# A two-layer attention and feed-forward kernel: late row vectors loaded early, column sums of the last weight moved one tile on, 40 idle products at the front

## The chip, the cores and the metric

The kernel runs on one core of one Trainium2 chip. A core has a matrix engine (PE, TensorE; its weight loads are shown apart as PEld), a vector engine (DVE), a scalar engine (ACT), a general engine (POOL, GpSimd) and a queue engine (SP) that issues DMAs. The engines run their own instruction lists side by side and wait for one another by semaphores. The metric is the device time of one execution in microseconds (us); lower is better.

## The reference

The input is 8 tiles of 128 tokens with 256 features, with a context of the same shape. Four blocks are added to it in turn, each on the layer-normalised input.

```python
x = x + _L0_xattn_ref(_layernorm(x), ctx, theta_w, ..., out_w, out_b)   # attention over 256 columns, latent 64
x = x + _L0_ffn_ref(_layernorm(x), w_gate, w_up, w_down)                # silu(gate)*up, Hadamard, 8-bit x ternary
x = x + _L1_xattn_ref(_layernorm(x), ctx, Wq, bq, Wkv, bkv, Wp, bp)     # 16 heads, 1024 queries x 1024 keys
x = x + _L1_ffn_ref(_layernorm(x), w1, b1, gamma, beta, w2, b2)

def _L1_ffn_ref(x, w1, b1, gamma, beta, w2, b2):
    h = bitlinear(x, w1, b1)
    h = jax.nn.gelu(h, approximate=False)
    h = layernorm(h, gamma, beta)          # gamma and beta are 1024 long
    return bitlinear(h, w2, b2)            # ternary w2
```

The rounded numbers of the last product carry an offset of 128. It is taken off with the column sums of the ternary W2, which have to be known before the last stage.

## The kernel before

Everything is kept in on-chip memory, and each engine has one instruction list in an order written out by hand. The stages follow one another, with some overlap:

- **First stage** (about 0 to 80 us): loads, first layer norm, first attention, and the key and value projections of the second attention from the context. `ctx_transposes(j)` turns the context of pair j of tiles (buffer `cx`), `project(j)` and `values1(j)` multiply the normalised input, `k_project` and `v_project` read the K/V weights (`wkvs`). GpSimd adds `xs` and `cx` in `x_plus_ctx`.
- **Gate stage** (about 80 to 125 us) and the Hadamard and down products that follow it. ACT sums and rounds the weights (`w_sums`, `w_round`), which come in through two slots of `stage`; SP issues the loads of w_down, w1 and w2 when a slot comes free (`sp.wait_ge(w_int, ...)`).
- **Second attention** (about 173 to 370 us): a loop over u from 0 to 127, u = 16 t + h for tile t and head h. For each u, PE computes the scores of 128 queries by 1024 keys in two products of 512 columns (`scores(u)`, L1928, once `exp` of u - 3 is done), DVE takes the negated maximum (`nm`, L1385), POOL makes the bias (`eb`, L581), ACT takes the exponential (L908). The result is turned either by a DMA transpose that SP issues (`turn(u)`, L402) or, for heads 1, 4, 12 and 15 of tiles 1 to 7, by PE (`round_transposes(u)`, L1940) and ACT (`move(u)`, L895). Seven heads later PE multiplies it with the values (`attend`, L1955). Query tiles are turned in between (`q_transposes`, L1725, and `qT_out`, L879): those of tile 7 at u = 17 through bank 7 (`N_BANK`), which the column sums and the PE transposes of the heads also use.
- **Last stage**: the wide product with W1, gelu, second layer norm with gamma and beta, the product with W2.

`wide_rows` holds b1, gamma and beta, 1024 numbers each, and is spread over all 128 partitions: 1.5 MB in on-chip memory. SP issues that one DMA in the attention loop, behind the turns up to u = 20 (L412), into a part of `rb` that the query quantisation has left. GpSimd reads b1 from u = 36 on (`b1_part`), DVE reads gamma and beta in the last stage.

The column sums of W2 are eight products on PE at u = `W2_SUMS` = 18 (L1845), behind a wait for `q_tr_sb` = 8, which is the copy of the last turned query tile on ACT. DVE scales them at u = 19 (`w2_correction`, L1424), and PE waits for that at u = 20 before it uses bank 7 again. The code of that part of the PE loop is this:

```python
                if u == W2_SUMS:
                    pe.wait_ge(q_tr_sb, T)
                    column_sums(W2, N_BANK, c2_ps)
                if u == H + ON_TENSOR[0] + TR_LAG:
                    pe.wait_ge(c2_sb, 1)
```

Of the kernel before, what the change touches and what calls it, by code (L numbers as in the profile page):

```python
# [23 lines left out]
P = 128  # L24
T = 8
NP = T // 2
D = 256
F = 1024
# [3 lines left out]
H = 16  # L32
# [14 lines left out]
TR_LAG = 3  # L47
# [7 lines left out]
T_BANK, D_BANK, N_BANK, Q_BANK = 4, 5, 7, 6  # L55
LATE_Q = {11: 5, 14: 6, 17: 7}
FIRST_ATTENDED = {9: (0, 1), 10: (2, 3), 11: (4,), 12: (5,), 13: (6,)}
W2_SUMS = 18
SUM_LAG = 3
PROJ_LAG = 14  # L60
O_OUT_LAG = 8
# [8 lines left out]
SUM_BANK, SCALE_BANK, XQ_BANK = 0, 2, 4  # L70
GATE_BANKS = (4, 5, 0, 1)
UP_BANKS = (6, 7, 2, 3)
ROWS = ["bq", "bk", "bp", "b2"]
WIDE_ROWS = ["b1", "gamma", "beta"]

# [44 lines left out]
def build(nc, x, ctx_in, att_w, out_w, gam_bet, cols, ident, hada, blk, rows, wide_rows, w_gate, w_up, w_down,  # L120
          wq, wkv, wp, w1, w2, out):
    with ExitStack() as stack:
# [82 lines left out]
        qz = [rb[:, 1024 * b:1024 * b + 1024].bitcast(BF16).rearrange("p (j e n) -> p j e n", e=2, n=P) for b in range(2)]  # L205
        osb = rb[:, 2048:4096].rearrange("p (t n) -> p t n", t=T)
        oT = rb[:, 7168:7680].rearrange("p (b c n) -> p b c n", b=2, c=2)
        wide = rb[:, 4096:7168]
        rowv.update({n: wide[:, F * i:F * i + F] for i, n in enumerate(WIDE_ROWS)})

        hw = [ra[:, F * t:F * t + F] for t in range(T)]
        squares = rb[:, 0:512].bitcast(BF16)
# [53 lines left out]
        def bank(b, n=1):  # L266
            return ps[:, b * 512:(b + n) * 512]
# [93 lines left out]
        def wslot(i):  # L361
            return stage[:, i % 2, :]
# [7 lines left out]
        @block.sync  # L370
        def _(sp):
            sp.dma_start(attw[:, :], att_w).then_inc(ld_att, 16)
            for j in range(NP):
                sp.dma_start(pair(xs, j), pair(x_d, j)).then_inc(ld_x[j], 16)
                sp.dma_start(pair(cx, j), pair(c_d, j)).then_inc(ld_c[j], 16)
            sp.dma_start(gb[:, :, :], gam_bet).then_inc(ld_const, 16)
            sp.dma_start(outw[:, :], out_w).then_inc(ld_const, 16)
            sp.dma_start(half_mean[:, :], blk).then_inc(ld_const, 16)
            sp.dma_start(wkvs[:, :, :], wkv).then_inc(ld_kvw, 16)
            sp.dma_start(h128[:, :], hada).then_inc(ld_const, 16)  # L380
            for i in range(2):
                sp.dma_start(wslot(i), w_d[i]).then_inc(ld_w[i], 16)
            sp.dma_start(wqs[:, :, :], wq).then_inc(ld_qpw, 16)
            sp.dma_start(wps[:, :, :], wp).then_inc(ld_qpw, 16)
            for i in range(2, 5):
                sp.wait_ge(w_int, i - 1)
                sp.dma_start(wslot(i), w_d[i]).then_inc(ld_w[i], 16)
            sp.wait_ge(qz_zero, 1)

            def pad_queries(t):  # L390
                sp.wait_ge(q_tr_sb, t + 1)
                if t >= 2:
                    sp.wait_ge(s_ps, H * (t - 1))
                for e in range(2):
                    r = slice(SLOT * e, SLOT * e + SLOT)
                    sp.dma_start(qz[t % 2][r, :, e, :], qT[r, t, :, :]).then_inc(q_pad[t % 2], 16)

            def turn(u):
                sp.wait_ge(s_exp, u + 1)
                if u >= R_RING:  # L400
                    sp.wait_ge(s_av, u - R_RING + 1)
                sp.dma_start_transpose(rT[u % R_RING].rearrange("p (c n) -> p c n", c=T),  # L402
                                       esc[u % E_RING].bitcast(F16)).then_inc(s_turned[u % R_RING], 16)

            pad_queries(0)
            pad_queries(1)
            for u in range(U):
                if not by_tensor(u):
                    turn(u)
                if u == H + 4:  # L410
                    sp.wait_ge(q_tr_sb, T)
                    sp.dma_start(wide, wide_rows.to_broadcast([P, wide.shape[1]])).then_inc(ld_wide, 16)  # L412
                if u % H == 1 and 2 <= u // H + 1 < T:
                    pad_queries(u // H + 1)
            for t in range(T):
                sp.wait_ge(f_out, t + 1)
                sp.dma_start(o_d[:, t, :], xn[:, t, :]).then_inc(out_done, 16)
            sp.wait_ge(out_done, 16 * T)
# [3 lines left out]
        def _(pool):  # L422
# [118 lines left out]
            def b1_part(step, piece):  # L541
# [1 line left out]
                c = slice(D * piece, D * piece + D)  # L543
                x, y = bwork[:, 0, :], bwork[:, 1, :]
                if step == 0:
                    pool.wait_ge(ld_wide, 16)
                    pool.wait_ge(w_tern, 5)
                    ins = nc.gpsimd.tensor_copy(bpart[:, c], rowv["b1"][:, c])
                elif step in (1, 4):
# [487 lines left out]
        def _(dve):  # L1037
# [432 lines left out]
            q_quant4(3)  # L1470
            for u in range(9, U + O_LAG):
                attention(u)
                if u == W2_SUMS + 1:
                    w2_correction()


# [54 lines left out]
            xqT_out(2, NP + 2, token_bank(2))  # L1531
            o_sums(T - 1)
            o_scale(T - 1)
            dve.wait_ge(ld_wide, 16)
            f_centre(0)
            f_scales(0)
            o_residual(T - 1)
# [28 lines left out]
        def _(pe):  # L1566
# [170 lines left out]
            def w_total(i, b):  # L1737

                pe.wait_ge(w_abs, i + 1)
                M(b[:, i:i + 1], ones[:, :], wsum[:, i:i + 1], start=True, stop=True).then_inc(w_tot, 1)  # L1740

            ctx_transposes(0)
            ctx_transposes(1)
            project(0)
            values1(0)
# [162 lines left out]
            def q_transposes(t):  # L1908
                n_bank_read()
                pe.wait_ge(q_four, t + 1)  # L1910
                head_transposes(t, q4[(t // 2) % 2], bank16(N_BANK), q_tr)
                in_n_bank[1] += 1
# [175 lines left out]
            for u in range(9, U + AV_LAG):  # L2088
                if u < U:
                    scores(u)  # L2090
                if u in LATE_Q:
                    q_transposes(LATE_Q[u])
                if u == W2_SUMS:
                    pe.wait_ge(q_tr_sb, T)
                    column_sums(W2, N_BANK, c2_ps)
                if u == H + ON_TENSOR[0] + TR_LAG:
                    pe.wait_ge(c2_sb, 1)
                if u - TR_LAG < U and by_tensor(u - TR_LAG):
                    round_transposes(u - TR_LAG)
# [100 lines left out]
```

## Time and profile before

| what | value |
|---|---|
| time, three runs | 419.59, 421.86, 423.8 us (median 421.86) |
| the profiled execution: its time | 422.52 us |
| the profiled execution: its span | 420.7 us |
| outside the span | 1.82 us |
| mean granted TensorE clock | 0.862 |
| busy: PE, DVE, ACT, POOL | 313.3, 350.7, 321.6, 126.0 us |

The span goes from the first to the last instruction of the core in one profiled execution. All durations below are from that execution. Busy time is a sum over the whole span. No engine is busy all the time, and each stage has its own limit, so it says little about one stage.

### The profile page before, as it was taken

How to read it: one execution, taken by the hardware profiler on the slowest of the kernel's cores; microseconds unless marked ns; L12 is line 12 of the kernel's file. 1: busy time of each engine (PE TensorE's matmuls, PEld its weight loads, DVE VectorE, ACT ScalarE, POOL GpSimd, SP SyncE). 2: the span in 40 equal slices, each digit the busy share in tenths (PEclk: the TensorE clock that was granted, in tenths of full speed). 3: DMA queues.
4: the chain of work that ended last, by engine and by line, in shares of the span. 5: the costliest groups of instructions: out<-in, count | busy, mean ns of one | idle time of the engine just before them, and what ended most of it. 6: DMA issues, size and time to landing. Idle time of an engine off the chain costs nothing.

```text
span 420.7 us, 7501 instructions
## 1 busy us (share of the span) xinstructions
PE 313.3 (74%) x2597; PEld 190.7 (45%) x2597; DVE 350.7 (83%) x562; ACT 321.6 (76%) x523; POOL 126.0 (30%) x303
## 2 busy tenths in 40 slices
PE   3989997674657698766587777777687766888967
PEld 2756554421256587444343444443444443533434
DVE  4658999379999888779588999989999999779885
ACT  2676689854205858979879998999999999887851
POOL 5333534200010220312211456532322232247330
PEclk9969999589558799888979997999989998995576
DMA  8800032000002002256989897989888978900001
GB/s 276 332 2 2 2 100 100 2 0 1 0 2 100 2 0 50 52 101 129 153 226 189 164 158 138 171 136 161 162 150 151 158 145 133 145 2 14 12 25 51
DMA packets 119862, 40.97 MB, mean 97 GB/s; under 512 B 114704, under 2 KB 118416, under 8 KB 119056
## 3 DMA queue, kind: packets, MB, share of 16 engines
q1 hardware_dynamic: 119392, 39.89, 47.4%
q8 instruction: 21, 0.34, 0.4%
q0 software_dynamic: 144, 0.52, 0.3%
q14 instruction: 17, 0.14, 0.1%
q10 hardware_dynamic: 288, 0.07, 0.1%
HBM read 11.11 MB, written 1.05 MB: 29 GB/s over the span
## 4 chain that ended last, share of the span: by engine, by line
DVE 27%; PE 25%; ACT 24%; issue 18%; DMA 3%; POOL 2%; SPq 0%; DVEq 0%; ACTq 0%; POOLq 0%
ACT rb L908 15%; DVE nm L1385 4%; PE ps L1928 3%; PE ps L2033 3%; PE ps L1990 2%; DVE rb L1303 2%; PE ps L1904 2%; PE ps L1940 2%; DVE gs L1294 2%; DMA tern<-rb 2%; DVE rb L1316 1%; DVE st L1048 1%; PE ps L1824 1%; DVE rb L1314 1%; PE ps L1835 1%
## 5 line engine op out<-in xcount | busy, mean ns | idle before, releaser
L1385 DVE TENSOR_REDUCE nm<-ps 128x1 f32<-128x1024 f32 x128 | 153.3, 1218 | 16.8 <-PE ps L1928 15.8
L908 ACT ACTIVATE rb<-ps,eb,sq 128x1024 int16<-128x1024 f32 x128 | 153.7, 1216 | 11.2 <-POOL eb L581 10.8
L1928 PE MATMUL ps<-ra,rb 128*128 128x512 bf16 x256 | 83.9, 413 | 43.4 <-ACT rb L908 42.8
L581 POOL TENSOR_SCALAR eb<-nm,sq 128x1 f32<-128x1 f32 x128 | 34.2, 267 | 126.4 <-DVE nm L1385 125.3
L1928 PEld LDWEIGHTS ps<-ra,rb 128*128 128x128 bf16 x256 | 15.8, 99 | 61.7 <-ACT rb L908 59.7
L1955 PEld LDWEIGHTS ps<-ra,tern 128*128 128x128 f16 x624 | 25.0, 98 | 16.8 <-issue 4.9
L1955 PE MATMUL ps<-ra,tern 128*128 128x16 f16 x624 | 25.8, 171 | 2.9 <-DVE rb L1123 2.3
L1824 PE MATMUL ps<-xqT,tern 128*128 128x512 bf16 x64 | 20.3, 464 | 9.8 <-DVE rb L1303 8.5
L908 ACT ACTIVATION_READ_ACCUMULATOR rb<-ps,eb,sq 128x1 f32 x128 | 27.3, 213 | 0.0
L771 ACT ACTIVATE sl<-gs 128x512 f32<-128x512 f32 x16 | 9.8, 626 | 17.6 <-DVE rb L1303 15.0
L1940 PEld LDWEIGHTS ps<-idh,rb 128*128 128x128 f16 x224 | 15.6, 106 | 16.1 <-issue 10.1
L1940 PE MATMUL ps<-idh,rb 128*128 128x128 f16 x224 | 19.0, 234 | 4.8 <-issue 2.5
L778 ACT ACTIVATE sB<-ps,shift,small 128x1024 uint8<-128x1024 f32 x8 | 9.6, 1204 | 15.4 <-DVE small L1334 15.4
L1955 PEld LDWEIGHTS ps<-ra,stage 128*128 128x128 f16 x400 | 16.0, 97 | 8.6 <-issue 1.1
L1294 DVE TENSOR_TENSOR gs<-ps,sB 128x512 f32<-128x512 f32 x16 | 11.0, 686 | 7.3 <-issue 5.1
L1824 PEld LDWEIGHTS ps<-xqT,tern 128*128 128x128 bf16 x64 | 6.2, 112 | 23.2 <-DVE rb L1303 14.6
L1955 PE MATMUL ps<-ra,stage 128*128 128x16 f16 x400 | 16.5, 170 | 0.0
L1835 PE MATMUL ps<-h,ra 128*128 128x128 f32 x64 | 10.9, 348 | 4.1 <-DVE ra L1316 4.1
L524 POOL TENSOR_SCALAR ve<-mv 128x2 f32<-128x2 f32 x4 | 1.3, 323 | 41.8 <-DVE mv L1051 41.8
L1725 PE MATMUL ps<-idb,rb 128*128 128x128 bf16 x128 | 11.0, 236 | 2.8 <-ACT ra L716 1.0
L1990 PE MATMUL ps<-tern,xqT 128*128 128x512 bf16 x32 | 13.1, 503 | 0.0
L1725 PEld LDWEIGHTS ps<-idb,rb 128*128 128x128 bf16 x128 | 8.9, 107 | 8.0 <-issue 4.6
(236 smaller groups left out, 727.9 us busy)
## 6 DMA issues: line engine op xcount, KB each, us to landing
stage<-w SPq DMA_DIRECT2D x2, 1024.0 KB, 4.7
rb<-ra SPq DMA_DIRECT2D x16, 128.0 KB, 2.9
rb<-wide_rows SPq DMA_DIRECT2D x1, 1536.0 KB, 7.1
xs<-x SPq DMA_DIRECT2D x4, 256.0 KB, 4.9
cx<-ctx_in SPq DMA_DIRECT2D x4, 256.0 KB, 5.2
stage<-w_gate SPq DMA_DIRECT2D x1, 1024.0 KB, 7.9
stage<-w_up SPq DMA_DIRECT2D x1, 1024.0 KB, 10.6
stage<-w_down SPq DMA_DIRECT2D x1, 1024.0 KB, 4.8
```

The source lines that it names most:

```text
L581: nc.gpsimd.tensor_scalar(eb[:, u % 3:u % 3 + 1], nm[:, u % 3:u % 3 + 1], sq[:, t, h:h + 1], LN255, ALU.mult, ALU.add).then_inc(s_bias, 1)
L908: A(esc[u % E_RING], bank(2 * (u % 3), 2), ACT.Exp, bias=eb[:, u % 3:u % 3 + 1], scale=sq[:, t, h:h + 1], accum_out=es[:, t % 2, h:h + 1]) ...
L1294: V.tensor_tensor(gs[:, n % 2, :], bank(GATE_BANKS[n % 4]), sB[:, 512 * hf:512 * hf + 512], ALU.mult).then_inc(g_scaled, 1)
L1385: V.tensor_reduce(nm[:, u % 3:u % 3 + 1], bank(2 * (u % 3), 2), AX.X, ALU.max, negate=True).then_inc(s_max, 1)
L1725: ins = TR(b[:, jj * P:jj * P + P], src[:, o:o + P], idb[:, :])
L1824: ins = M(bank(b[n % 4]), tern[:, w, F * k + P * c:F * k + P * c + P], xqT[:, k, 512 * hf:512 * hf + 512], start=(k == 0), stop=(k == 1))
L1835: ins = M(bank(2 * (t % 2), 2)[:, P * c:P * c + P], mixes[hf][:, c, P * (t % 4):P * (t % 4) + P], h128[:, :], start=True, stop=True)
L1928: ins = M(bank(2 * (u % 3) + hf), qz[t % 2][:, h // 2, h % 2, :], kT[:, h // 2, 512 * hf:512 * hf + 512], start=True, stop=True)
L1940: ins = TR(half_bank(7)[:, P * c:P * c + P], esc[u % E_RING].bitcast(F16)[:, P * c:P * c + P], idh[:, :])
L1955: ins = M(bank(6)[:, HD * h:HD * h + HD], rT[u % R_RING][:, P * c:P * c + P], vq[:, c, HD * h:HD * h + HD], start=(c == 0), stop=(c == T - 1))
L1990: ins = M(b, xqT[:, k, P * t:P * t + P], tern[:, W1, F * k + 512 * hf:F * k + 512 * hf + 512], start=False, stop=(k == 1))
L2033: ins = M(b, fT16[:, t % 2, P * c:P * c + P], w[:, D * c:D * c + D], start=False, stop=(c == FC - 1))
```

## The change

It does three things.

1. The DMA of `wide_rows` is taken out of the attention loop and split in two. b1 goes to `wkvs`, once the key and value projections are done; gamma and beta go to `cx`, once the context has been turned, added and projected. SP issues both directly behind the load of w_down and ahead of that of w1, with five waits. The readers wait for 32 instead of 16 on `ld_wide` and read from the new places.
2. `W2_SUMS` goes from 18 to 43, head 11 of tile 2. The wait for `q_tr_sb` moves to u = 20, where the wait for `c2_sb` stood; that wait moves to u = 47. The sums wait for the copy of the turned attention output of tile 1 (`o_tr_sb` = 2). DVE scales them at u = 46, behind the residual of tile 1.
3. Ahead of the first context transposes PE does 34 products of a 128 by 128 matrix of ones with itself into bank 5, which nothing reads, and 6 more between the first and the second pair.

```diff
-W2_SUMS = 18
+W2_SUMS = 43
...
+SPARE_BANK = 5
...
-        wide = rb[:, 4096:7168]
-        rowv.update({n: wide[:, F * i:F * i + F] for i, n in enumerate(WIDE_ROWS)})
+        wide_b1 = wkvs[:, :, :].rearrange("p k n -> p (k n)")
+        wide_gb = cx[:, :, :].rearrange("p t d -> p (t d)")
+        rowv.update({"b1": wide_b1, "gamma": wide_gb[:, 0:F], "beta": wide_gb[:, F:2 * F]})
...
             for i in range(2, 5):
                 sp.wait_ge(w_int, i - 1)
                 sp.dma_start(wslot(i), w_d[i]).then_inc(ld_w[i], 16)
+                if i == 2:
+                    sp.wait_ge(v_ps, 4)
+                    sp.wait_ge(k_ps, NP)
+                    sp.dma_start(wide_b1, wide_rows[:, 0:F].to_broadcast([P, F])).then_inc(ld_wide, 16)
+                    sp.wait_ge(xc_set, NP)
+                    sp.wait_ge(a_g, NP)
+                    sp.wait_ge(c_t, NP)
+                    sp.dma_start(wide_gb, wide_rows[:, F:3 * F].to_broadcast([P, 2 * F])).then_inc(ld_wide, 16)
...
-                if u == H + 4:
-                    sp.wait_ge(q_tr_sb, T)
-                    sp.dma_start(wide, wide_rows.to_broadcast([P, wide.shape[1]])).then_inc(ld_wide, 16)
...
-                if u == W2_SUMS + 1:
+                if u == W2_SUMS + 3:
                     w2_correction()
...
+            def keep_busy(n):
+
+                for i in range(n):
+                    M(bank(SPARE_BANK)[:, 0:P], one16[:, :], one16[:, :], start=True, stop=True)
+
+            pe.wait_ge(shift_set, 1)
+            keep_busy(34)
             ctx_transposes(0)
+            keep_busy(6)
             ctx_transposes(1)
...
+                if u == H + ON_TENSOR[0] + TR_LAG:
+                    pe.wait_ge(q_tr_sb, T)
                 if u == W2_SUMS:
-                    pe.wait_ge(q_tr_sb, T)
+                    pe.wait_ge(o_tr_sb, u // H)
                     column_sums(W2, N_BANK, c2_ps)
-                if u == H + ON_TENSOR[0] + TR_LAG:
+                if u == W2_SUMS + 4:
                     pe.wait_ge(c2_sb, 1)
```

PE's list at u = 18 and 19, before. The products `ps<-ra,rb` are scores, `ps<-ra,tern` are attended heads, `ps<-tern,one` the column sums.

```order
L1928 MATMUL ps<-ra,rb 128x512 [waits s_exp]
L1928 MATMUL ps<-ra,rb 128x512
L1845 MATMUL ps<-tern,one 1x256 [waits shift_set,w_tern,q_tr_sb]
L1845 MATMUL ps<-tern,one 1x256 x7
L1955 MATMUL ps<-ra,tern 128x16 [waits s_turned1]
L1955 MATMUL ps<-ra,tern 128x16 x7
L1928 MATMUL ps<-ra,rb 128x512 [waits s_exp]
```

The same place after:

```order
L1943 MATMUL ps<-ra,rb 128x512 [waits s_exp]
L1943 MATMUL ps<-ra,rb 128x512
L1970 MATMUL ps<-ra,tern 128x16 [waits s_turned1]
L1970 MATMUL ps<-ra,tern 128x16 x7
L1943 MATMUL ps<-ra,rb 128x512 [waits s_exp]
```

The eight sums and their wait are gone from between two pairs of scores. PE's list at u = 43 and 44, after:

```order
L1943 MATMUL ps<-ra,rb 128x512 [waits s_exp]
L1943 MATMUL ps<-ra,rb 128x512
L1860 MATMUL ps<-tern,one 1x256 [waits shift_set,w_tern,o_tr_sb]
L1860 MATMUL ps<-tern,one 1x256 x7
L1970 MATMUL ps<-ra,stage 128x16 [waits s_moved]
L1970 MATMUL ps<-ra,stage 128x16 x7
L1943 MATMUL ps<-ra,rb 128x512 [waits s_exp]
```

They stand here now, again between two pairs of scores; before, nothing stood between the second and the fifth of these rows. SP's list from the load of w_down on, after:

```order
L389 DMA stage<-w_down 128x2048 [waits w_int]
L393 DMA wkvs<-wide_rows 128x1024 [waits k_ps,v_ps]
L397 DMA cx<-wide_rows 128x2048 [waits c_t,a_g,xc_set]
L389 DMA stage<-w 128x2048 [waits w_int] x2
L406 DMA rb<-ra 64x8x128 [waits q_tr_sb,qz_zero]
```

Both new loads stand ahead of the loads of w1 and w2; before, the first and the fourth row were neighbours.

## Rows read from the trace of the kernel before

**Rows 1.** Profile page: busy engines; the chain that ended last, by engine.

```profile
PE 313.3 (74%) x2597; PEld 190.7 (45%) x2597; DVE 350.7 (83%) x562; ACT 321.6 (76%) x523; POOL 126.0 (30%) x303
DVE 27%; PE 25%; ACT 24%; issue 18%; DMA 3%; POOL 2%; SPq 0%; DVEq 0%; ACTq 0%; POOLq 0%
```

**Rows 2.** Timeline at u = 18 to 20: start, us, engine, line, what, [idle before].

```profile
206.99 1.07 ACT L879 ACTIVATE ra<-ps 128x1024 bf16<-128x1024 bf16 x1
207.89 1.26 ACT L908 ACTIVATE rb<-ps,eb,sq 128x1024 int16<-128x1024 f32 x1
208.11 1.03 PE L1845 MATMUL ps<-tern,one 128*1 128x256 f16 x8 [2.68 <-ACT ra L879]
...
209.29 0.84 PE L1928 MATMUL ps<-ra,rb 128*128 128x512 bf16 x2
...
210.17 1.23 DVE L1385 TENSOR_REDUCE nm<-ps 128x1 f32<-128x1024 f32 x1 [3.48 <-PE ps L1928]
...
211.47 0.35 DVE L1424 TENSOR_SCALAR half_mean<-ps 1x256 f16<-1x256 f32 x1
...
211.79 1.20 ACT L908 ACTIVATE rb<-ps,eb,sq 128x1024 int16<-128x1024 f32 x1 [2.55 <-POOL eb L581]
...
211.88 1.04 PE L1940 MATMUL ps<-idh,rb 128*128 128x128 f16 x8 [0.68 <-DVE half_mean L1424]
```

**Rows 3.** Timeline: exponentials of heads 6 and 14 of tile 1.

```profile
216.83 1.20 ACT L908 ACTIVATE rb<-ps,eb,sq 128x1024 int16<-128x1024 f32 x1
...
227.85 1.20 ACT L908 ACTIVATE rb<-ps,eb,sq 128x1024 int16<-128x1024 f32 x1 [0.62 <-POOL eb L581]
```

**Rows 4.** Timeline: exponentials of heads 2, 6 and 14 of tile 2.

```profile
233.64 1.21 ACT L908 ACTIVATE rb<-ps,eb,sq 128x1024 int16<-128x1024 f32 x1
...
238.84 1.24 ACT L908 ACTIVATE rb<-ps,eb,sq 128x1024 int16<-128x1024 f32 x1
...
249.26 1.20 ACT L908 ACTIVATE rb<-ps,eb,sq 128x1024 int16<-128x1024 f32 x1
```

**Rows 5.** DMA issues of the page (KB, median us to landing).

```profile
rb<-wide_rows SPq DMA_DIRECT2D x1, 1536.0 KB, 7.1
```

**Rows 6.** The DMA transposes (L402): time to landing.

```profile
DMA to landing us min/median/max: 3.1/3.3/6.4
```

**Rows 7.** Timeline of SP and PE behind the issue of the wide load at 214.40.

```profile
216.96 9.31 SPq L402 DMA_TRANSPOSE tern<-rb  x5
...
224.87 0.36 PE L1955 MATMUL ps<-ra,tern 128*128 128x16 f16 x8 [0.59 <-DMA tern<-rb]
```

**Rows 8.** Timeline at u = 44 to 47: PE, DVE.

```profile
244.55 0.60 PE L1928 MATMUL ps<-ra,rb 128*128 128x512 bf16 x2 [0.67 <-ACT rb L908]
...
245.19 3.60 DVE L1385 TENSOR_REDUCE nm<-ps 128x1 f32<-128x1024 f32 x3 [0.23 <-PE ps L1928]
```

**Rows 9.** Timeline of the first 13 us.

```profile
1.09 0.20 POOL L445 MEMSET one<- 128x128 f16 x1
...
6.25 1.09 PE L1676 MATMUL ps<-idf,cx 128*128 128x128 f32 x4 [6.25 <-DMA cx<-ctx_in]
...
7.76 1.09 PE L1676 MATMUL ps<-idf,cx 128*128 128x128 f32 x4 [0.42 <-DMA cx<-ctx_in]
...
8.78 1.12 PE L1580 MATMUL ps<-cx,attw 128*64 128x256 f32 x4
...
...
12.21 0.42 DVE L1064 COPY sB<-ps 128x256 f32<-128x256 f32 x1 [1.17 <-PE ps L1592]
```

**Rows 10.** Windows of 5 us: busy time of PE, PEld, DVE, ACT, POOL; PEclk; DMA share; GB/s.

```profile
25.00:30.00 5.00, 5.00 (x16) 3.41 (x14) 1.45 (x4) 2.58 (x10) 2.48 (x2) 0.52 0.01 3
...
210.00:215.00 5.00, 4.32 (x44) 2.31 (x43) 3.76 (x5) 2.97 (x5) 0.53 (x2) 0.50 0.72 131
```

**Rows 11.** Timeline: end of the last key projection; first use of w1.

```profile
66.83 1.13 PE L1718 MATMUL ps<-wkvs,rb 128*128 128x256 f32 x4
...
96.30 1.89 ACT L691 ACTIVATE tern<-stage 128x2048 bf16<-128x2048 f32 x1
```

More of the change, by code:

```diff
@@ L545, in b1_part @@
                 if step == 0:
-                    pool.wait_ge(ld_wide, 16)
+                    pool.wait_ge(ld_wide, 32)
                     pool.wait_ge(w_tern, 5)
@@ L1533, in _ @@
             o_scale(T - 1)
-            dve.wait_ge(ld_wide, 16)
+            dve.wait_ge(ld_wide, 32)
             f_centre(0)
```

## Prediction

> **What bounds the kernel now.** I read the page first. DVE is busy 83% of the span, ACT 76%, PE 74%, and the chain that ended last is shared by DVE, PE and ACT [rows 1]. So no engine bounds the whole, and the change touches three places. Each has to be read where it stands.
>
> The second attention is a stream of exponentials on ACT. The reader can measure a tile by the starts of the same heads. In tile 2, heads 2 to 14 start at 233.64 and 249.26, which is 15.62 us for twelve heads with two moves for PE's turns among them [rows 4]. In tile 1 the same heads start at 207.89 [rows 2] and 227.85 [rows 3], which is 19.96 us. The work is the same, so tile 1 loses 19.96 - 15.62 = 4.34 us between its heads 2 and 14. That is exactly the stretch with the column sums and the wide load.
>
> The timeline says how. PE has done the scores of u = 18 and stands for 2.68 us, until ACT has copied the last turned query tile (206.99 plus 1.07), and only then does the eight sums, 208.11 to 209.14. The scores of u = 19 come at 209.29 and take 0.84 us where a pair takes 0.60 at another place [rows 2, 8]. DVE stands for 3.48 us, ACT for 2.55 us; exponential 19 starts 3.90 us behind exponential 18. PE then waits once more, for DVE's scaled sums (0.68 us), and its granted clock is 0.50 in the window from 210 to 215, the lower of its two levels, 1.2 GHz [rows 2, 10].
>
> **The sums leave u = 18.** Heads 2 to 6 take 216.83 - 207.89 = 8.94 us in tile 1 and 238.84 - 233.64 = 5.20 us in tile 2 [rows 2 to 4]. The difference of 3.74 us is the wait, the sums, the second wait and the slow clock behind them. What is late next? The scores of u = 19 need exponential 16, which was over before the copy of 206.99 began, so they follow within half a microsecond of those of u = 18. DVE takes up their maximum behind that of 18. ACT's list has copy, exponential 18, exponential 19, which makes ACT itself the next limit, as in tile 2. The wait for the copy stands now ahead of PE's turn at u = 20. Queued behind it are the attended head and the scores of 21, whose release is exponential 18, over at 207.89 + 1.26 = 209.15; the copy is over at 208.06. So the moved wait costs nothing, and I take the whole 3.74 us. From below: if only ACT's own hole of 2.55 us closed, 2.6.
>
> **The wide load leaves the loop.** Heads 6 to 14 take 227.85 - 216.83 = 11.02 us in tile 1, 249.26 - 238.84 = 10.42 us in tile 2 [rows 3, 4]. The difference is 0.60 us. It is the wait of PE for a turned head at 224.87 (0.59 us), which ACT repeats as 0.62 us [rows 3, 7]. A DMA transpose lands after 3.3 us in the middle and 6.4 us at most [rows 6], and the longest stands behind the wide load, 1.5 MB with 7.1 us to landing [rows 5]. Gain 0.60; bounds 0 (the transposes stay late, see the rivals) and 0.60.
>
> **Where the load goes.** SP is in order, so behind its new waits stand the loads of w1 and w2. The last wait to be met is that for the key projection, whose products end at 66.83 + 1.13 = 67.96 [rows 11]. The two new loads together are as large as the old one; if they took its 7.1 us and w1 as much again behind them, w1 would be there at about 83 us with the issues. ACT first reads it at 96.30 [rows 11]. The load of w2 waits for a much later rounding. SP's list has no transpose before the second attention, so no head waits for these bytes. Cost nothing; the cover is the 13 us ahead of 96.30, and without it the gate stage would wait for what is missing. The readers of b1, gamma and beta change only their source buffer.
>
> **The sums arrive at u = 43.** Eight sums took 1.03 us [rows 2]. Ahead of the scores of u = 44 PE stands idle for 0.67 us, waiting for ACT [rows 8]. That hides 0.67, and 1.03 - 0.67 = 0.36 us is left. DVE stood idle 0.23 us ahead of that maximum because of PE and then runs three maxima without a hole [rows 8], so it has nothing to hide 0.36 with. At u = 46 it also gets the scaling, 0.35 us [rows 2], ahead of the maximum of 47; PE's turn at 47 waits for it, and behind that turn are an attended head and the scores of 48. The wait for `o_tr_sb` is met: that copy came on ACT at u = 40, and the scores of 43 already need exponential 40. Bounds 0 (ACT has slack at the move) and 0.36 + 0.35 = 0.71. I take 0.5, nearer to the upper end, since DVE ran without a hole there.
>
> **The 40 products at the front.** The ones are written at 1.09 + 0.20, the first context pair lands at 6.25, so PE has 5.0 us to itself [rows 9]. No row shows such products; the nearest is eight turns of 128 columns in f16 at the lower clock, 1.04 us, 0.13 each [rows 2]. 34 of them take 4.4 us and end at 5.8 us, ahead of 6.25. The six in between take 0.8 us at the lower clock; PE stands there 0.42 us for the second context pair anyway [rows 9], so they could delay it by 0.4 us. What can they bring? The four turns at 6.25 and at 7.76 took 1.09 us each, and the projection at 8.78 took 1.12 us: these are slow. DVE stands for 1.17 us at 12.21 because PE is late [rows 9], and that is all that the path can win here, for DVE's own list limits it next. So the bounds are a gain of 1.2 and a loss of 0.4. Against the full gain speaks that the clock does not stay: the kernel of before has it fall again in the window from 25 to 30 (0.52) although PE is busy there [rows 10], after a stretch with holes, and the front keeps a hole between 5.8 and 6.25 and one ahead of the projection. I take a gain of 0.3.
>
> **The sum.** 3.74 + 0.60 - 0.5 + 0.3 = 4.1 us off. The profiled execution took 422.52 us with a span of 420.7; that gives 418.4 and a span of 416.6. It stood 0.66 above the median of 421.86. Against the median the forecast is **417.8 us**.
>
> **Rivals.** (a) The transposes become the limit once tile 1 runs at ACT's pace. For it: five of them took SP 9.31 us, 1.86 each [rows 7], more than an exponential every 1.2 to 1.3 us, of which 12 in 16 go to SP. Against it: that was behind the wide load, and a head has seven heads' time until it is needed, over 8 us, against 3.3 to landing. Ten transposes late by 0.6 each, less 4.5 us of slack, give back 1.5 us: 419.3. The Trainium skill, page "DMA: Bandwidth & Descriptors", section "Latency and other measured facts", gives 261 GB/s for a DMA transpose; as an estimate from that page, one head of 0.26 MB would take 1.0 us, under the pace of ACT, which speaks against this rival; no run here shows the rate by itself.
>
> (b) The clock goes the other way in its favour. The front and the earlier stream shift PE's busy stretches, and the fall at 25 to 32 us does not come. There PE is busy 5.00 of 5 us [rows 10] and what it does would shrink by some 2 of them; with the front's 1.2 in place of 0.3 the sum is 4.1 + 0.9 + 1 = 6.0: 415.9. The same with the other sign, a fall more in the attention or the last stage and 1.5 us lost, gives 419.3.
>
> (c) Slower than before: each product of ones waits for the one ahead, since all write the same place of bank 5, and all 40 hold up the context. With p for one product, the projection starts at 1.3 + 40 p + 2 x 1.09 in place of 8.78, so the delay is 40 p - 5.3. It eats the other 3.8 us from p = 0.23 on; at 0.30 it is 6.7 us and the result 424.7. Against it: the eight sums, which all go to one place in one bank, took 0.13 each [rows 2]. The Trainium skill, page "TensorE: Matmul & The Clock Gate", section "Back-to-back issue gap", has 107 ns for 128 columns at the lower clock; by it the 34 end at 5.0 us.
>
> (d) The front does nothing at all, since the clock is low again before the projection. That is the forecast with 0 in place of 0.3: 418.1.
>
> **How the numbers follow.** Forecast with (d) 0.56, over 416.6 to 419.0 from the bounds of the terms; (a) 0.14; (b) 0.18 in its favour and 0.08 against; (c) 0.04. A measurement of this kernel can tell about 1% from no change, here 4.2 us, and the forecast lies on that edge. A little under half of the first and nearly all of (b)'s first half are faster by over 1%: 0.44. Slower by over 1% is (c) with its worst half and little more: 0.04. The rest, 0.52, is within 1%. The runs of before lie 4.2 us apart, which widens what a median of few can be. The range is 415.3 to 420.8.
>
> **What would show it.** Right: exponential 19 starts 1.2 us behind 18, heads 2 to 14 of tile 1 take about 15.6 us, the transposes land in 3.3 us at most 4; in tile 2 the same heads take 15.9 to 16.3; DVE copies its first `sB` between 11.0 and 12.2; w1 lands ahead of 85. Wrong: PE waits for transposes at u = 25 to 30 (a); the first context turn starts behind 6.3 (c); a granted clock of 0.5 in the first attention or in the second attention where it was 1.00 (b).

## The result, and the profile after

The changed kernel took 415.75 us (median of four runs, 413.77 to 417.2) beside 421.95 for the kernel before, a ratio of 0.990 with a 95% interval of 0.985 to 0.995. The forecast was 417.8, with a range of 415.3 to 420.8. Twelve more runs of the same kernel, six on each of two other chips and beside the kernel before on the same chip, gave a median of 413.61 (ratio 0.985, 0.981 to 0.9885) and 414.58 (0.986, 0.981 to 0.990), so the change is worth 6 to 7 us by the medians and 1.0 to 1.5% by the ratios. The medians here and below count every run, while the ratios leave out runs over 1.5% above the fastest of their kernel (at the extreme 449.96 us for e4 below and 820.84 us for the kernel before, both unexplained), so the two can differ.

The profiled execution of after took 417.2 us with a span of 415.4. The busy times and the chain of its page, beside [rows 1]:

```profile
PE 308.1 (74%) x2637; PEld 191.4 (46%) x2637; DVE 351.1 (85%) x562; ACT 321.6 (77%) x523; POOL 126.2 (30%) x303
DVE 31%; ACT 26%; PE 20%; issue 18%; POOL 3%; DMA 1%; SPq 0%; DVEq 0%; ACTq 0%; POOLq 0%
```

The work is the same, with 40 products more on PE. What changed is whom the chain passes: PE fell from 25% to 20% and DMA from 3% to 1%, while DVE and ACT rose.

**Tile 1 of the attention.** The timeline of after, the exponentials 18, 19, 22 and 30 and what PE does between the first two; the columns are start, us, engine, line, what, [idle before]:

```profile
207.73 1.07 ACT L886 ACTIVATE ra<-ps 128x1024 bf16<-128x1024 bf16 x1
...
207.94 0.60 PE L1943 MATMUL ps<-ra,rb 128*128 128x512 bf16 x2 [0.40 <-ACT rb L915]
...
208.63 1.26 ACT L915 ACTIVATE rb<-ps,eb,sq 128x1024 int16<-128x1024 f32 x1
...
208.85 0.62 PE L1955 MATMUL ps<-idh,rb 128*128 128x128 f16 x8 [0.31 <-ACT ra L886]
...
209.81 1.27 ACT L915 ACTIVATE rb<-ps,eb,sq 128x1024 int16<-128x1024 f32 x1
...
213.84 1.29 ACT L915 ACTIVATE rb<-ps,eb,sq 128x1024 int16<-128x1024 f32 x1
...
224.25 1.19 ACT L915 ACTIVATE rb<-ps,eb,sq 128x1024 int16<-128x1024 f32 x1
```

Exponential 19 starts 1.18 us behind 18, where it was 3.90 [rows 2]. PE waits 0.31 us for the copy, now ahead of its turn, and ACT, DVE and SP all run on. Heads 2 to 6 take 213.84 - 208.63 = 5.21 us and heads 2 to 14 take 15.62, where it was 8.94 and 19.96 [rows 2, 3].

**Tile 2.** Its heads 2 to 14 went from 15.62 [rows 4] to 16.47 us in this execution (230.02 to 246.49). The granted clock fell to 0.50 from 234.0 to 237.4 there, so this trace does not price the sums; the second and third traces of the same kernel do, below.

**The new loads.** The page has them with 4.2 and 6.3 us to landing. They were issued at 70.3 and 70.8, and w1 at 71.2; the slowest of the loads of w_down, w1 and w2 took 8.4 us, so w1 was there by 79.6, and ACT first read it at 93.5.

**The front** did not help in this execution. The timeline of after, first 16 us:

```profile
1.36 3.81 PE L1752 MATMUL ps<-one 128*128 128x128 f16 x34 [1.36 <-POOL one L452]
...
5.28 0.63 PE L1683 MATMUL ps<-idf,cx 128*128 128x128 f32 x4
5.75 0.50 PE L1752 MATMUL ps<-one 128*128 128x128 f16 x6
...
8.03 0.63 PE L1683 MATMUL ps<-idf,cx 128*128 128x128 f32 x4 [1.79 <-DMA cx<-ctx_in]
9.01 1.12 PE L1587 MATMUL ps<-cx,attw 128*64 128x256 f32 x4 [0.35 <-DVE xn L1064]
...
12.92 0.42 DVE L1071 COPY sB<-ps 128x256 f32<-128x256 f32 x1 [1.55 <-PE ps L1599]
...
16.27 1.23 DVE L1075 TENSOR_REDUCE nmax<-ps 128x4 f32<-128x1024 f32 x1 [1.64 <-PE ps L1611]
```

34 products take 3.81 us, 0.112 each, so the products of ones do not wait for one another. The context turns that follow take 0.63 us in place of 1.09 [rows 9]: PE works at its upper rate. Then it stands for 1.79 us until the second context pair has landed, and from 9.01 on the first projection takes 1.12 us again. The windows say what the granted clock was (columns: stretch, us, PE busy, instructions, granted clock, DMA share, GB/s):

```profile
8.00:10.00 2.00, 1.62 (x10) 0.66 1.15 371
10.00:12.00 2.00, 2.00 (x11) 0.50 1.00 394
12.00:14.00 2.00, 2.00 (x11) 0.50 1.04 435
14.00:16.00 2.00, 2.00 (x12) 0.63 1.01 426
```

At 0.50, 1.2 GHz, DVE copies `sB` at 12.92, later than before, and takes its first score maximum at 16.27, where the kernel before has it at 14.32:

```profile
14.32 1.22 DVE L1068 TENSOR_REDUCE nmax<-ps 128x4 f32<-128x1024 f32 x1 [0.39 <-PE ps L1604]
```

Exponential 0 starts at 174.88 in place of 173.00. This execution lost 1.9 us there. It won its time in tile 1 and in the last stage: from exponential 127 to the end it took 54.15 us, where before took 56.93. The second of these can't be put down to the change: that stage, whose list is the same in all kernels here but for the place of gamma and beta, took 52.5 to 56.9 us, and 56.9 as well in the changed kernel without its third part (e1).

### The profile page after: what moved, and what is told of

The parts are those of the page before. It is cut to its first block, busy times and chain, and to the rows that moved or that the text cites. A ratio compares the mean times of both kernels' runs of the same rounds, so it can differ in the third digit from the quotient of the medians.

```text
span 415.4 us, 7585 instructions
## 1 busy us (share of the span) xinstructions
PE 308.1 (74%) x2637; PEld 191.4 (46%) x2637; DVE 351.1 (85%) x562; ACT 321.6 (77%) x523; POOL 126.2 (30%) x303
## 4 chain that ended last, share of the span: by engine, by line
DVE 31%; ACT 26%; PE 20%; issue 18%; POOL 3%; DMA 1%; SPq 0%; DVEq 0%; ACTq 0%; POOLq 0%
ACT rb L915 18%; DVE nm L1392 4%; PE ps L1943 3%; DVE rb L1310 2%; PE ps L1839 2%; DVE gs L1301 2%; PE ps L2048 2%; PE ps L1919 2%; DVE rb L1323 1%; DVE st L1055 1%; PE ps L1955 1%; DVE small L1337 1%; DVE rb L1321 1%; DVE ra L1497 1%; DMA xs<-x 1%
## 5 line engine op out<-in xcount | busy, mean ns | idle before, releaser
L1943 PE MATMUL ps<-ra,rb 128*128 128x512 bf16 x256 | 81.1, 401 | 47.5 <-ACT rb L915 46.9
L1970 PE MATMUL ps<-ra,stage 128*128 128x16 f16 x400 | 16.5, 170 | 0.0
L1850 PE MATMUL ps<-h,ra 128*128 128x128 f32 x64 | 12.0, 374 | 4.1 <-DVE ra L1323 4.1
L1850 PEld LDWEIGHTS ps<-h,ra 128*128 128x128 f32 x64 | 11.7, 288 | 4.1 <-issue 4.1
L2014 PE MATMUL ps<-idh,sB 128*128 128x128 f16 x56 | 5.7, 262 | 9.2 <-ACT sB L992 9.2
```

The source lines that it names most:

```text
L1850: ins = M(bank(2 * (t % 2), 2)[:, P * c:P * c + P], mixes[hf][:, c, P * (t % 4):P * (t % 4) + P], h128[:, :], start=True, stop=True)
L1943: ins = M(bank(2 * (u % 3) + hf), qz[t % 2][:, h // 2, h % 2, :], kT[:, h // 2, 512 * hf:512 * hf + 512], start=True, stop=True)
L1970: ins = M(bank(6)[:, HD * h:HD * h + HD], rT[u % R_RING][:, P * c:P * c + P], vq[:, c, HD * h:HD * h + HD], start=(c == 0), stop=(c == T - 1))
```

## The experiments

Twelve kernels on three chips: e1 to e4 on one, e5 to e8 on a second, e9 to e12 on a third. The kernel before ran beside them with a median of 421.05 (35 runs), 420.15 (17) and 421.86 us (17). "nmax" is the start of the first score maximum of the first attention, "exp 0" that of exponential 0; tiles are heads 2 to 14. These four columns are from the one profiled execution of each kernel, so a number in them is one execution and no mean.

| kernel | median us (runs) | ratio [95%] | nmax | exp 0 | tile 1 | tile 2 |
|---|---|---|---|---|---|---|
| before | 421.86 (3) | | 14.32 | 173.00 | 19.96 | 15.62 |
| after | 415.75 (4) | 0.990 [0.985, 0.995] | 16.27 | 174.88 | 15.62 | 16.47 |
| e1, no front | 417.38 (12) | 0.992 [0.988, 0.995] | 16.37 | 174.66 | 15.55 | 15.87 |
| e2, sums alone | 420.75 (12) | 0.9935 [0.9884, 0.9985] | 16.45 | 174.88 | 18.96 | 16.45 |
| e3, load alone | 420.92 (12) | 1.0015 [0.998, 1.005] | 14.73 | 173.46 | 19.23 | 16.20 |
| e4, front alone | 419.14 (12) | 0.995 [0.991, 0.9993] | 12.37 | 168.67 | 23.10 | 16.22 |
| e5, holes filled | 414.63 (6) | 0.988 [0.984, 0.9915] | 14.99 | 171.55 | 15.55 | 15.87 |
| e6, sums twice | 414.51 (6) | 0.985 [0.981, 0.989] | 12.23 | 170.28 | 15.56 | 16.74 |
| e7, after again | 413.61 (6) | 0.985 [0.981, 0.9885] | 12.27 | 168.86 | 15.65 | 15.86 |
| e8, load in tile 3 | 418.01 (12) | 0.991 [0.987, 0.995] | 12.71 | 172.52 | 15.61 | 16.31 |
| e9, load in tile 4 | 419.68 (10) | 0.993 [0.988, 0.997] | 12.65 | 171.82 | 15.54 | 15.79 |
| e10, no front again | 417.10 (6) | 0.990 [0.985, 0.994] | 16.28 | 174.78 | 15.56 | 15.87 |
| e11, after, third | 414.58 (6) | 0.986 [0.981, 0.990] | 12.73 | 171.71 | 15.58 | 15.88 |
| e12, sums at 59 | 416.60 (6) | 0.988 [0.984, 0.993] | 13.00 | 171.22 | 15.56 | 15.63 |

### Each part alone (e1 to e4)

e1 is the change without its third part:

```diff
-            pe.wait_ge(shift_set, 1)
-            keep_busy(34)
             ctx_transposes(0)
-            keep_busy(6)
             ctx_transposes(1)
```

e2 is the kernel before with the second part alone, `W2_SUMS = 43` and its waits. e3 is before with the first part alone, the two early loads. e4 is before with the 40 products alone.

> The change without the 40 products of ones. Theory A (the stretch of tile 1 carries the gain: 3.74 us by the sums, 0.60 by the load, the front is worth nothing on the whole): 1.0% under the kernel before, 417.6 us, heads 2 to 14 of tile 1 in 15.6 us, and the first exponential of the second attention about 1.9 us earlier than in the trace of the changed kernel (174.88). Theory B (the front is worth about 2 us and is part of the result): only 0.6% under, 419.5 us.

> The kernel before with the column sums at u = 43 and nothing else. Theory A: heads 2 to 14 of tile 1 take 15.6 us plus what the wide load holds up, 16.2; heads 2 to 14 of tile 2 take 16.0 in place of 15.62; 0.8% under the kernel before, 418.5 us. Theory C (the load is the stall, the sums only stand where it shows): tile 1 stays above 18 us and the time within 0.3% of before. With the load still in the loop and the heads at full pace, the transposes could also be later than in the kernel before (rival (a)): then heads 6 to 14 of tile 1 take over 11.5 us.

> The kernel before with b1, gamma and beta loaded in the gate stage and nothing else. Theory A: exponential 19 still starts 3.9 us behind 18, heads 6 to 14 of tile 1 take 10.4 in place of 11.02 us, no transpose lands later than 5.5 us; 0.15% under the kernel before, 421.3 us, which the timing can't tell from none. Theory C: 3 us or more off.

> The kernel before with the 40 products of ones and nothing else. Theory A: within 0.4% of before (422 us); where the granted clock falls to 0.5 behind the products, the first score maximum comes later than 14.32 us, where it stays up, at 13.2. Theory B: 0.4% or more under, 420 us. A loss of up to 2 us is possible as well: in the trace of the changed kernel the clock is up at 5.3, falls at 8.7 and stays down to 15.5, and the first score maximum is at 16.27.

The prediction priced the sums at 3.74 us and the wide load at 0.60. In these traces, alone, the sums bring 19.96 - 18.96 = 1.00 us and the load 0.73, and together 4.31 to 4.41. The times say as much of e3 (ratio 1.0015) and leave e2 open (median 0.3 us under before, ratio 0.9935). Heads 2 to 6 of e2 do take 5.20 us, as said; its heads 6 to 14 then take 13.76 in place of 11.02. The timeline of e2, exponentials 18, 22 and 30 and what stands between:

```profile
209.90 1.25 ACT L908 ACTIVATE rb<-ps,eb,sq 128x1024 int16<-128x1024 f32 x1
...
214.48 0.58 SPq L412 DMA_DIRECT2D rb<-wide_rows  x1
215.10 1.28 ACT L908 ACTIVATE rb<-ps,eb,sq 128x1024 int16<-128x1024 f32 x1
...
216.91 8.10 SPq L402 DMA_TRANSPOSE tern<-rb  x3
...
222.44 0.36 PE L1955 MATMUL ps<-ra,tern 128*128 128x16 f16 x8 [0.98 <-DMA tern<-rb]
...
224.96 0.36 PE L1955 MATMUL ps<-ra,tern 128*128 128x16 f16 x8 [1.20 <-DMA tern<-rb]
...
228.86 1.20 ACT L908 ACTIVATE rb<-ps,eb,sq 128x1024 int16<-128x1024 f32 x1 [2.15 <-POOL eb L581]
```

The three transposes in the fourth row hold SP for 8.10 us: the first for 4.38, the second for 2.27, and the third is back at 1.26. The slowest lands after 8.0 us. ACT delivers a head every 1.3 us, so PE waits twice for a turned head, 2.18 us, and ACT stands for 2.15. That is the rival (a) of the prediction, in the kernel that keeps the load. In e3 the other cause stays: exponential 19 starts 3.88 us behind 18 and the free queue brings little. So in these traces each cause hides behind the other in part. How large that part is stays open, for the granted clock was 0.50 from 225.4 to 228.8 in e2; with the price of the load where the clock stayed at 1.00 (1.76 us, e9 below) the sums alone would bring some 2.6 us and not 1.00, as an estimate.

e4 has the list of before in tile 1, word for word, and takes 23.10 us there in place of 19.96. The granted clock fell to 0.50 at 201.6 to 205 and 218.6 to 228.8, exponential 19 starts 4.86 us behind 18, heads 6 to 14 take 14.04 us, and PE stands for 1.72 us for a turned head. So the 19.96 of before is one execution too, and the load can cost more than 0.60 us with the sums still at u = 18.

e1 has no front and the same tile 1 as the change, so the 4.3 us are the first two parts' alone. Its time, 417.38, is what theory A said (417.6), but its trace is not: exponential 0 starts at 174.66 and not 1.9 us ahead of 174.88. So the time of e1 does not show that the front is worth nothing; the next section prices it. e4 came out 1.9 us under before (ratio 0.995), on the side of its theory B.

### The front (e5, e7, e10, e11)

e7 and e11 are the changed kernel, e10 is e1 again. e5 fills the two holes in which PE stood in the trace of after:

```diff
             ctx_transposes(0)
-            keep_busy(6)
+            keep_busy(24)
             ctx_transposes(1)
+            keep_busy(6)
             project(0)
```

> The changed kernel as it is, once more, beside the kernel before on the same chip. Its ratio was 0.990 from four runs. By what the runs so far show (stretch of tile 1 worth 4.3 us, sums at u = 43 a cost of 0.3 to 0.5, front products 0 to 2 by the clock that follows them): 416.5 to 417.5 us, ratio 0.989 to 0.991. If the 2 us that parted the change with and without the products of ones were chance, it comes out with the kernel without them, ratio 0.992. The first attention is read again: either the raised clock is lost at about 9 us, as in the first trace of this kernel (exponential 0 at 174.9), or it stays to about 24 us as in the kernel that has the products alone (exponential 0 at 168.7). If both are seen with one and the same list of instructions at the front, what decides is when the clock's steps fall and not the kernel.

> The change with more products of ones: 24 in place of 6 between the first and the second context pair, and 6 new ones ahead of the first projection, so that PE stands nowhere between 1.4 and 9 us. Theory A (the clock falls at about 9 us because PE stood for 1.8 and 0.35 us just ahead): the raised clock stays in every execution, project(0) runs at 1.00, exponential 0 starts at 169 to 172 in place of 174.9, and the time is 1 to 3 us below that of the change, 413.5 to 416. Price if the clock is still low at the first context turns: 18 products more of 0.107 us are 1.9 us against a wait for the DMA of 1.8, so nothing. Theory B (what decides is the phase of the steps): the time is that of the change within 1 us, 416 to 417.5, and the clock is lost or kept as before.

> The change without the 40 products of ones, this time on one chip with the change itself, which prices the products. From the two calls before, 417.4 us without them (ratio 0.992) and 413.6 with them (ratio 0.985): 0.7% or 2.9 us. Theory A (the products are worth about 2 us because the clock is high in the first products): this kernel is 1.5 to 3.5 us above the change. Theory B (they are worth 0.3 as forecast, the rest is chance and chip): within 1 us of it. In the trace exponential 0 starts at 173 to 175.

> The changed kernel as it is, as the partner of the other three: 413.5 to 416 us, ratio 0.985 to 0.989. A third trace of the front: exponential 0 was at 174.88 in the first and at 168.86 in the second. Between those if the first context pair lands between 5.0 and 6.5 us and the clock is up by the projection.

e7 came out 3 us below what I had expected of it (416.5 to 417.5). e10 and e11 on one chip give the price: 417.10 against 414.58, 2.5 us, which is theory A of e10. The six runs of each overlap (415.53 to 418.03, and 413.63 to 417.01) and their means lie 1.9 us apart, so the size is known to a microsecond or so. The timeline of e10 without the products:

```profile
5.14 1.09 PE L1683 MATMUL ps<-idf,cx 128*128 128x128 f32 x4 [5.14 <-DMA cx<-ctx_in]
...
8.42 1.12 PE L1587 MATMUL ps<-cx,attw 128*64 128x256 f32 x4
...
12.23 1.12 PE L1587 MATMUL ps<-cx,attw 128*64 128x256 f32 x4
...
16.15 0.73 PE L1587 MATMUL ps<-cx,attw 128*64 128x256 f32 x4
16.28 1.23 DVE L1075 TENSOR_REDUCE nmax<-ps 128x4 f32<-128x1024 f32 x1 [2.23 <-PE ps L1611]
```

And the same of e7, the changed kernel, which has the list of after word for word:

```profile
4.95 1.06 PE L1683 MATMUL ps<-idf,cx 128*128 128x128 f32 x4
5.81 0.85 PE L1752 MATMUL ps<-one 128*128 128x128 f16 x6
...
7.99 0.65 PE L1587 MATMUL ps<-cx,attw 128*64 128x256 f32 x4 [0.39 <-DVE xn L1064]
...
12.27 1.21 DVE L1075 TENSOR_REDUCE nmax<-ps 128x4 f32<-128x1024 f32 x1
```

The same four projections take 1.12 or 0.65 us. Without the products the first fast ones come at 12.1 (before), 12.5 (e3) or between 16.2 and 17.1 us (e1, e2, e10); with the 34 and 6 they come at 7.5 to 8.7 in seven traces of eight, and the eighth is the one shown for after, where the rate was up at 5.28 and lost again at 9.01. The first score maximum starts at 15.63 on average in the five traces without the products and at 13.03 in the eight with them (of one form each, e5 aside), exponential 0 at 174.2 and 171.2. So 2.6 of the 2.9 us are won ahead of that first maximum. Up to 0.4 of them may be chance of the loads: PE starts the turn of the second context pair when it has landed, at 7.67 us on average in the five and at 7.26 in the eight.

Theory A of e5 falls as a way to gain. Its rate stays up from 9.86 on, but its first context pair landed only at 6.54, its 24 products then ran at the lower rate up to 9.66 us (22 of them start 0.107 us apart) and the second context pair, whose turn had begun between 6.6 and 8.1 us in the other traces, was turned at 9.86. The first maximum is at 14.99. Its time is 1.0 us above e7's, within what the runs tell apart. One trace can't say whether more products make the upper rate surer; here they delayed the context.

### Where the wide load costs (e8, e9)

Both are the change with the single load of 1.5 MB back in the loop, in the old place in `rb`, but in a later tile; GpSimd's parts of b1 start at u = 70 and 86 for it. The edit of e8 (e9 has `4 * H + 4`):

```diff
+                if u == 3 * H + 4:
+                    sp.wait_ge(q_tr_sb, T)
+                    sp.dma_start(wide, wide_rows.to_broadcast([P, wide.shape[1]])).then_inc(ld_wide, 16)
```

> The change, but with the wide load (one DMA of 1.5 MB into the old place) in the attention loop behind the turns of u = 52, in tile 3, instead of in the gate stage; the parts that GpSimd makes of b1 start at u = 70 for it. Theory A (a load on the queue of the transposes costs about 3 us wherever ACT runs at its own pace, as it did at u = 20 in the kernel with the sums moved alone, where heads 6 to 14 took 13.8 us in place of 10.4): heads 2 to 14 of tile 3 take 18.5 to 19 us in place of 15.6, transposes land after up to 8 us, and the time is 3 us above that of the change, 419.5 to 420.5. Theory B (it costs only where the query tiles are turned as well and heads are late already): tile 3 takes 15.6 to 16.4 and the time is within 1 us of that of the change.

> The same as the kernel with the wide load in tile 3, but behind the turns of u = 68, in tile 4, and GpSimd's parts of b1 from u = 86 on. In tile 3 heads 2 to 14 took 16.61 us with the load and 16.63 without, but four heads take 6.16 us at that place of tile 3 in any kernel, against 5.20 in tiles 1 and 4, so the queue had time to catch up. Theory A (what decides is the pace of the heads behind the load): tile 4 runs at ACT's pace as tile 1 does with the sums moved, so the load costs there what it cost at u = 20: heads 2 to 14 take 18 to 19 us in place of 15.55, with PE waiting for turned heads for 2 us in all. Theory B (what decides is tile 1 itself, where transposes are late for another reason): heads 2 to 14 of tile 4 take 15.55 to 16.0 us.

In tile 3 heads 2 to 14 take 269.03 - 252.42 = 16.61 us, and 16.63 in the kernel before: the load costs nothing there, although two transposes behind it took SP 5.28 us. Tile 3 holds a layer norm, and its heads run slower than ACT's pace there: the four behind the load, 53 to 57, take 6.02 us with it and 5.94 without (e10). Neither theory of e8 had tile 3 right (18.5 to 19, or 15.6 to 16.4), since both left the layer norm out; what came out is theory B's cost of nothing. In tile 4, with no layer norm, the same load shows (e9: exponential 66, the load, the two waits, exponential 78):

```profile
273.62 1.21 ACT L909 ACTIVATE rb<-ps,eb,sq 128x1024 int16<-128x1024 f32 x1
...
277.65 0.57 SPq L413 DMA_DIRECT2D rb<-wide_rows  x1
...
280.43 7.68 SPq L403 DMA_TRANSPOSE tern<-rb  x3
...
285.61 0.36 PE L1964 MATMUL ps<-ra,stage 128*128 128x16 f16 x8 [0.48 <-DMA stage<-rb]
...
287.95 0.36 PE L1964 MATMUL ps<-ra,tern 128*128 128x16 f16 x8 [1.01 <-DMA tern<-rb]
...
290.93 1.20 ACT L909 ACTIVATE rb<-ps,eb,sq 128x1024 int16<-128x1024 f32 x1 [1.05 <-POOL eb L582]
```

17.31 us, 1.76 more than the 15.55 of before, with the granted clock at 1.00 through that stretch. PE waits 1.49 us for turned heads. So the pace of the heads decides, and theory A of e9 has the mechanism; its size was half to 0.7 of the 2.5 to 3.5 us expected. In e2 the same mechanism cost 13.76 - 10.41 = 3.35, of which a part is the clock, at 0.50 from 225.4 to 228.8.

The times do not fit this alone: by the medians e8 is 4.4 us above e7 and e9 is 5.1 above e11, by the ratios 2.5 and 3.0, where the traces show 0 and 1.76. In the profiled execution of e8 the loop is 4.1 us longer than e7's; 2.2 of that stand in tile 0, which is far ahead of the load, and 1.7 in heads 92 to 94, where the granted clock was 0.50 from 308.2 to 315.0. Whether a load in the loop brings more such falls, or these were chance, stays open; so does whether GpSimd's later parts of b1, the second difference of e8 and e9, have a share.

### The sums at u = 43 (e6, e12)

e6 does the eight products twice, the second pass over the first; e12 moves the sums to head 11 of tile 3.

```diff
                 if u == W2_SUMS:
                     pe.wait_ge(o_tr_sb, u // H)
+                    for c in range(FC):
+                        M(bank(N_BANK)[0:1, 0:D], one16[:, 0:1], tern[:, W2, :].bitcast(F16)[:, D * c:D * c + D], start=(c == 0), stop=(c == FC - 1))
                     column_sums(W2, N_BANK, c2_ps)
```

> The change with the eight column sums at u = 43 done twice (the second pass overwrites the first, all else is the same), which prices them: the pass itself is about 1.0 us on PE, or half of it if the clock is high. Theory A (PE has a hole of 0.67 us ahead of the scores of u = 44 that the first pass fills, so the second lies bare): heads 2 to 14 of tile 2 take 17.0 to 17.5 us in place of 16.5, time 0.5 to 1.0 above that of the change, 417.0 to 418.5. Theory B (ACT has slack at that place and the first pass costs next to nothing, the rest of tile 2's loss is the clock): under 0.3 us more, tile 2 at 16.0 to 16.7 and no difference in the time.

> The change with the column sums at u = 59, the same head one tile on, in tile 3, whose heads 2 to 14 take 16.63 us in every trace, 1.1 more than ACT's own pace. Theory A (ACT and PE have slack in a tile with a layer norm in it): tile 2 comes back to 15.6 from 15.87 and tile 3 stays at 16.63, so 0.25 us less in all, which the time can't show: within 1 us of the change. Theory B (at head 11 tile 3 too runs at ACT's pace, the slack lies in its heads 2 to 6): tile 3 takes 16.9, tile 2 15.6, nothing gained.

Four traces with the sums at 43 and no fall of the clock in tile 2 (e1, e7, e10, e11) give 15.86 to 15.88 us for heads 2 to 14 and 21.86 to 21.88 for the whole tile, exponential 32 to 48, against 15.62 and 21.40 before. So the sums cost 0.25 and, with the scaling, 0.47 us. The timeline of e11 has both halves:

```profile
237.39 1.03 PE L1860 MATMUL ps<-tern,one 128*1 128x256 f16 x8
...
239.20 3.53 DVE L1392 TENSOR_REDUCE nm<-ps 128x1 f32<-128x1024 f32 x3 [0.48 <-PE ps L1943]
...
242.98 0.40 DVE L1431 TENSOR_SCALAR half_mean<-ps 1x256 f16<-1x256 f32 x1
...
243.44 0.62 PE L1955 MATMUL ps<-idh,rb 128*128 128x128 f16 x8 [0.58 <-DVE half_mean L1431]
```

DVE's hole ahead of the three maxima was 0.23 us [rows 8] and is 0.48. The other 0.22 come behind the scaling. In e6 that hole is 1.35:

```profile
234.66 1.03 PE L2113 MATMUL ps<-tern,one 128*1 128x256 f16 x8
...
237.35 3.52 DVE L1392 TENSOR_REDUCE nm<-ps 128x1 f32<-128x1024 f32 x3 [1.35 <-PE ps L1943]
```

Again 0.87 us more, and tile 2 takes 16.74 - 15.87 = 0.87 more. The first pass lies mostly in PE's hole, the second bare: theory A. The time, 0.9 above e7's, agrees but could not show it. Tile 2 stayed under the 17.0 to 17.5 us expected, which were reckoned from the 16.5 of the disturbed first trace. In e12 tile 2 is back at 15.63 and tile 3 takes 16.88 for 16.63, and 24.25 for 23.77 as a whole: the same 0.25 and 0.48. The cost moves with the sums, theory B. Neither e12 nor e5 beats the change.

## Why the prediction was right, and where it was not

- **The sums leave u = 18, 3.74, and the wide load leaves the loop, 0.60.** The sum of 4.34 was measured to the hundredth (19.96 to 15.62), and heads 2 to 14 took 15.55 to 15.65 in e1, e7, e10 and e11 as well. That it fits so closely is in part luck: both ends of the forecast are read from the one trace of before, and e4 took 23.10 us with the same list. The split was wrong. I read heads 2 to 6 as the sums' and heads 6 to 14 as the load's, but alone they bring 1.00 and 0.73 (e2, e3). With the stream at ACT's pace the load costs 1.8 us (e9), and 3.3 in e2 with a fall of the clock in it; the 0.60 of before was no bound.
- **"The moved wait costs nothing"** held: PE waits 0.31 us for the copy and exponential 19 follows in 1.18.
- **The signs.** Two that were named for a right forecast did not show: `sB` was first copied at 12.92 in after (11.0 to 12.2 said), and the slowest transpose of the changed kernel landed after 4.8 to 5.4 us (at most 4 said). The heads stayed at ACT's pace all the same.
- **Where the load goes, 0.** Held. w1 was in by 79.6 us against a forecast of 83, well ahead of its first use.
- **The sums at u = 43, 0.5** (bounds 0 to 0.71): 0.47. The mechanism was as said, part in PE's hole, part behind the scaling.
- **The front, 0.3** (bounds 1.2 gained to 0.4 lost): this is the step that failed, by about 2 us. Measured 2.5 us in time and 2.9 at exponential 0. The false sentence is "that is all that the path can win here". I took DVE's hole of 1.17 us at 12.21 [rows 9] from one execution in which PE's rate rose by 12.1 us. In three of five traces without the products it rose at about 16, where DVE's hole ahead of the first maximum is 2.23 us (e10) in place of 0.39 and two more sets of projections run slow. I also argued that the clock does not stay because it falls at 25 to 30 us. It does fall in every trace, with or without the products, first at 22 to 32 us (in after at 8.7 and then at 36); but what is gained ahead of that is kept.
- **The rivals.** (a) is not in the change and is real in e2; its 1.86 us for each transpose was a mean over one of 2.90, one of 2.14 and three of about 1.3, so it was a short stall and not a pace. (b) had the time nearly right, 415.9, and half of its reason: the rate at the front is worth more, while the fall at 25 to 32 us comes all the same, or a little earlier or later; its other half happened too, as the first trace of after shows, and is outweighed in the others. (c) falls: 34 products in 3.81 us are 0.112 each, half of the 0.23 from which it would have decided. The Trainium skill, page "TensorE: Matmul & The Clock Gate", section "Back-to-back issue gap", has 107 ns; the trace agrees within the tail of the last product. (d) falls with the 2.5 us.
- **The sum.** 4.34 - 0.47 + 2.5 gives 6.4, against 6.2, 6.5 and 7.3 us measured. With the forecast's 0.3 it was 4.1, which the range made up for: its low end came from rival (b). Two of the three medians of the changed kernel, 413.61 and 414.58, lie below that low end of 415.3; taken as ratios of 421.86 they give 415.5 and 415.8, just inside.

## What to carry to other kernels

Two causes in one stretch are not priced by cutting the stretch in two: take each out alone, since the one that looks small may only be hidden by the other. Here they were worth 1.00 and 0.73 alone and 4.3 together, with the clock in part of that. Before a hole in one execution is taken as the most that a change can win, ask whether that execution was a lucky one: here the first maximum came between 14.32 and 16.45 us in the five traces without the products, a spread of 2.1 us, larger than the bound of 1.2 read from the best of them. The large load was free behind heads that ran slower than ACT's pace (e8), and cost 1.8 us behind heads at that pace (e9).

## What the runs showed of the hardware

**The granted clock has no record at the start.** These are windows of e10:

```profile
0.00:4.00 4.00, 0.00 (x0) 1.00 0.51 150
8.00:10.00 2.00, 2.00 (x11) 1.00 1.06 364
10.00:12.00 2.00, 2.00 (x10) 1.00 1.08 419
12.00:14.00 2.00, 2.00 (x10) 1.00 1.04 438
```

The granted clock reads 1.00 in all of them, in the first too, in which PE did nothing, and the projections in the others took 1.12 us, as those of after did at 0.50, and not 0.65. The 1.00 is no measurement: each trace holds records of the clock only from its first rise on, and a window without a record is printed as 1.00. The first records stand at 11.5 us (before), 12.0 (e3), 16.4 (e1, e10) and 17.0 (e2), against 4.4 to 7.0 in the eight traces with the 34 and 6 products and 9.7 in e5, and the fast products begin there. Ahead of the first record, the time of one product is what shows the rate. In the first trace of after the clock rose at 5.2 and fell to 0.50 at 8.7, once PE had stood for 1.79 us and worked for 0.63; PE then stood for 0.35 and was busy throughout until the clock rose again at 15.5.

**The same list has its clock fall in different places from run to run.** Of after, e7 and e11, which are one kernel, exponential 0 starts at 174.88, 168.86 and 171.71, and the falls inside the attention stand at 234, 255 (after), 246, 273, 280 (e7) and 250, 261 us (e11) among others. Such falls went with losses of 0 to 2.1 us: heads 2 to 14 of tile 3 took 18.71 in e11 and 16.63 in e7. A stage in one trace should be compared with the same stage in several before a microsecond of it is explained.

**A broadcast load of 1.5 MB holds up the transposes behind it.** The slowest landed after 8.0 us (e2) and 7.5 (e9), where 3.3 is the median. It is one stall and not a slower pace: the second transpose behind the load held SP for 4.38 us (e2), 4.01 (e9) and 3.62 (e8), the next for 2.27, 2.23 and 1.26, and after that each took about 1.3 again.
